# Moving the seams between MLP pieces and attention work in a two-layer transformer kernel

## The reference, cut to what matters

```python
# x: 32 x 64 tokens of 512 (seen as 2048 tokens, 16 tiles of 128); cond: one vector for each of the 32 entries
def layer0(x):
    h = ada_rms(x, cond, ln1)              # x * rsqrt(mean(x^2)) * w * (1 + cond @ tw.T)
    q, k, v = h @ Wq.T, h @ Wk.T, h @ Wv.T # 8 heads of 64, one shared key and value head; rope on q and k
    x = x + softmax(q k^T / 8) v @ Wo.T    # attention inside an entry of 64 tokens
    h = ada_rms(x, cond, ln2)
    return x + (silu(h @ Wg.T) * (h @ Wu.T)) @ Wd.T        # inner width 2048
def layer1(x):
    h = layernorm(x) * (1 + scale(cond)) + shift(cond)
    q = h @ Wq.T; k, v = (h @ Wkd.T) @ Wku.T, (h @ Wkd.T) @ Wvu.T    # 16 heads of 32, 4 key heads, rope
    return x + softmax(q k^T / sqrt(32)) v @ Wo.T
out = layer1(layer0(x))
```

## Time and profile before

| | us |
|---|---|
| median of 3 runs | 886.98 (885.87 to 887.53) |
| the profiled execution, its own time | 887.57 |
| its span from first to last instruction | 885.7 |
| PE busy | 852.0 |
| DVE busy | 631.7 |
| ACT busy | 447.2 |
| POOL busy | 406.6 |

### The profile page before, as it was taken

How to read it: one execution, slowest core, us unless ns; L and a number is a source line. 1 busy time by engine, 2 the same in 40 slices (tenths; PEclk the granted TensorE clock), 3 DMA queues, 4 the chain that set the end, 5 groups by cost and what they waited for, 6 DMA issues and landing times.

```text
span 885.7 us, 15530 instructions
## 1 busy us (share of the span) xinstructions
PE 852.0 (96%) x5864; PEld 707.2 (80%) x5864; DVE 631.7 (71%) x1005; ACT 447.2 (50%) x821; POOL 406.6 (46%) x304
## 2 busy tenths in 40 slices
PE   9798999999999999999989899999999999999997
PEld 6686888788788888787878678788888888888885
DVE  6686577677666677677546877887877867868886
ACT  4665444544444444445445564563553654644662
POOL 2456445545545545537444644544534534431331
PEclk9899999999999999999999899999999999999999
DMA  9811535435425435334423446355354354330001
GB/s 348 330 32 37 172 99 159 124 110 160 122 87 168 122 104 154 116 99 151 156 96 90 169 122 185 115 166 156 121 164 139 114 175 142 117 102 13 25 27 36
DMA packets 114298, 113.54 MB, mean 128 GB/s; under 512 B 57520, under 2 KB 80048, under 8 KB 114224
## 3 DMA queue, kind: packets, MB, share of 16 engines
q1 hardware_dynamic: 113504, 112.45, 39.8%
q10 hardware_dynamic: 720, 0.09, 0.1%
HBM read 88.15 MB, written 24.38 MB: 127 GB/s over the span
## 4 chain that ended last, share of the span: by engine, by line
PE 65%; DVE 11%; ACT 9%; issue 8%; POOL 6%; POOLq 0%; DVEq 0%; ACTq 0%
PE ps L643 20%; PE ps L645 19%; PE ps L644 19%; PE ps L757 2%; POOL gul L511 2%; ACT yf L1763 1%; PE ps L918 1%; ACT L1643 1%; POOL wdl L516 1%; DVE al L1247 1%; DVE ex L1232 1%; PE ps L689 1%; DVE af L1265 1%; ACT ah L1710 1%; ACT guh L1688 1%
## 5 line engine op out<-in xcount | busy, mean ns | idle before, releaser
L511 POOL TENSOR_TENSOR gul<-rgu,guh 128x1024 fp32r<-128x1024 f32 x64 | 154.3, 2411 | 217.5 <-ACT guh L1688 217.5
L1252 DVE TENSOR_TENSOR xres<-ps,xres 128x512 f32<-128x512 f32 x256 | 174.3, 687 | 67.3 <-PE ps L645 67.3
L643 PE MATMUL ps<-h2h,guh 128*128 128x512 f32 x512 | 205.0, 400 | 2.1 <-issue 2.1
L645 PE MATMUL ps<-h2l,guh 128*128 128x512 f32 x512 | 200.6, 392 | 0.0
L644 PE MATMUL ps<-h2h,gul 128*128 128x512 f32 x512 | 200.2, 391 | 0.0
L643 PE MATMUL ps<-wdh,ah 128*128 128x512 f32 x256 | 102.3, 399 | 14.7 <-DVE al L1247 14.7
L643 PEld LDWEIGHTS ps<-h2h,guh 128*128 128x128 f32 x512 | 96.5, 189 | 23.1 <-issue 2.5
L645 PEld LDWEIGHTS ps<-h2l,guh 128*128 128x128 f32 x512 | 96.5, 188 | 21.1
L1710 ACT CAST ah<-af 128x512 fp32r<-128x512 f32 x64 | 39.8, 621 | 143.8 <-DVE af L1265 138.2
L644 PEld LDWEIGHTS ps<-h2h,gul 128*128 128x128 f32 x512 | 96.5, 189 | 19.6
L644 PE MATMUL ps<-wdh,al 128*128 128x512 f32 x256 | 100.7, 393 | 0.0
(11 more groups left out here) (180 smaller groups left out, 1655.5 us busy)
## 6 DMA issues: line engine op xcount, KB each, us to landing
rgu<-gu SPq DMA_DIRECT2D x64, 512.0 KB, 3.9
rwd<-WdT SPq DMA_DIRECT2D x64, 256.0 KB, 3.7
turned_q<-tq SPq DMA_DIRECT2D x20, 320.0 KB, 2.3
qkT<-turned_q SPq DMA_DIRECT2D x20, 320.0 KB, 3.7
turned_p<-tp SPq DMA_DIRECT2D x9, 512.0 KB, 2.6
pT<-turned_p SPq DMA_DIRECT2D x9, 512.0 KB, 3.8
xt<-xT SPq DMA_DIRECT2D x16, 256.0 KB, 2.7
out<-xres SPq DMA_DIRECT2D x15, 256.0 KB, 4.1
```

The lines of the kernel that those rows point to most:

```text
L511: pool.tensor_tensor(gul[i][:, :], rgu[i][:, :], guh[i][:, :], ALU.subtract).then_inc(m_gul, 1)
L643: pe.matmul(dst, lh, rh, start=start, stop=False)
L645: return pe.matmul(dst, lh, rl, start=False, stop=stop)
L1252: dve.tensor_tensor(at, bank(BD[i % 2]), at, ALU.add).then_inc(m_x, 1)
```

## The change

`FILL0[5]` becomes (2, 4, 4) and `FILL1[9]` becomes (4, 0, 0, 0, 0), so each step's work stands two pieces earlier in the order of pieces, and the order across a seam becomes C D | A B. In layer 1, `stats1` moves to the end of the step before, `mean_rstd` to the middle of the first fill on DVE, `rstd1` to the head of the step on POOL, and softmax's scaling and `turn_probs1` behind the whole first fill. `turn_y` goes before `add_x` and `add_out`. The norm of the next MLP tile (`rstd2`, `square2`, `mean_sq2`, `norm2`), `scale_h2` and the trio `scale_shift_y`, `high_y`, `low_y` move before the fourth fill (`norm2` behind it). Layer 0's loop itself is as before, SP's too.

```diff
-FILL0 = {s: (4, 4, 4) for s in range(5, 16)}
-FILL1 = {-1: (4, 4, 0, 4, 0), **{u: (4, 2, 2, 2, 2) for u in range(0, 9)}, 9: (2, 0, 0, 0, 0)}
+FILL0 = {5: (2, 4, 4), **{s: (4, 4, 4) for s in range(6, 16)}}
+FILL1 = {-1: (4, 4, 0, 4, 0), **{u: (4, 2, 2, 2, 2) for u in range(0, 9)}, 9: (4, 0, 0, 0, 0)}
...
@@ POOL, layer 1
-                fill(pieces, min(f1, 2))
                 if u < TAIL:
                     rstd1(u + 2)
-                fill(pieces, f1 - min(f1, 2))
+                fill(pieces, f1)
...
                 fill(pieces, f2 + f3)
-                fill(pieces, f4)
+                if soon is not None:
+                    rstd2(soon)
                 if in_layer(u + 2):
                     low_y(u + 2)
+                fill(pieces, f4)
                 if ready is not None:
                     low_h2(ready)
-                if soon is not None:
-                    rstd2(soon)
                 if u == -1:
                     low_w1_out()
...
@@ DVE, end of layer 0's loop
+                if s == NT - 1:
+                    stats1(1)
@@ DVE, layer 1
-                if u < TAIL:
-                    stats1(u + 2)
                 fill(pieces, min(f1, 2))
                 if in_layer(u):
                     softmax_sums1(u)
+                if u < TAIL:
+                    mean_rstd(u + 2)
+                fill(pieces, f1 - min(f1, 2))
                 if 0 <= u <= TAIL:
                     softmax_scale1(u)
                 if 0 <= u < TAIL:
                     turn_probs1(u)
-                if u < TAIL:
-                    mean_rstd(u + 2)
-                fill(pieces, f1 - min(f1, 2))
...
+                if u < TAIL:
+                    turn_y(u + 2)
                 if u == -1:
                     add_x(NT - 1)
                 if in_layer(u - 1):
                     add_out(u - 1)
-                if u < TAIL:
-                    turn_y(u + 2)
...
-                fill(pieces, f4)
                 if ready is not None:
                     scale_h2(ready)
                 if soon is not None:
                     mean_sq2(soon)
+                fill(pieces, f4)
+                if u < TAIL:
+                    stats1(u + 3)
                 fill(pieces, f5)
                 if u == TAIL - 1:
-                    stats1(u + 3)
                     mean_rstd(u + 3)
@@ ACT, layer 1
-                fill(pieces, f4)
+                if soon is not None:
+                    square2(soon)
                 if u < TAIL:
                     scale_shift_y(u + 2)
                     high_y(u + 2)
+                fill(pieces, f4)
                 if ready is not None:
                     high_h2(ready)
                 if soon is not None:
-                    square2(soon)
+                    norm2(soon)
                 if u == -1:
                     high_w1_out()
                 fill(pieces, f5)
-                if soon is not None:
-                    norm2(soon)
```

## The result

The kernel after takes 896.14 us (median of 5 runs, 892.34 to 901.74) where the kernel before takes 886.63 us in 5 runs beside them. The ratio is 1.0123, 95% interval 1.0077 to 1.0169: slower, and 2.1 us above the upper end of the range. The profiled execution took 896.14 us with a span of 894.3 us, so 8.6 us of span have to be found.

The account below looks back on a forecast made before the run. PE was busy 852.0 of 885.7 us, leaving only its waits and slow clock to win. Terms 4.0 + 0.8 - 0.8 - 1.2 + 0.6 - 2.5 - 0.4 = +0.5 us took the median from 886.98 to 887.5; range 881.5 to 894.

Parts of the forecast that it names:

- Layer 0: Layer 0's eight steps with a norm: late norm makes 9.4 us of 5.3, +4.0 us, and late probabilities add 0.8.
- first rival: Layer 0: the late norm is no loss and the 5.3 us come back, giving 878.2 us; chance 0.1.
- the probabilities: Layer 0's eight steps: their write goes behind weight loads and lands after 4.5 us, 0.1 us a step, +0.8 us.
- third rival: Layer 0: probabilities land later behind the weights, PE waits 1 us per step at the context, 894.7 us; chance 0.15.
- s = 15 and u = -1: Last seam of layer 0 and the one after: less idle PE, -0.8 us at s = 15, -1.2 at u = -1.
- u = 0: Layer 1 seam: waits at gate, additions and context plus a likely clock fall, 7.5 us for 6.9, +0.6 us.
- u = 1 and 2: Layer 1 seams: no `w1` work and `stats1` out of the way, 1.0 us lost for 3.6, -2.5 us.
- u = 3: Layer 1 from this step on: PE is full and the Silu still ends before the next gate, 0 us.
- fourth rival: Layer 1 from u = 1 on: the y chain misses the gate, 0.7 us in 7 steps, 892.4 us; chance 0.12.
- u = 9: Layer 1's tail step: `qkv1(10)` waits less for `af` of the last unit, -0.4 us.

Follow-up runs that it names:

- e3: The kernel after with layer 0's `rstd2` before the last piece of the step (before its `gul`) on GpSimd; ratio 0.9978 to the kernel before, span 882.9 us.
- e4: The kernel after with layer 1's four transfers of turned y and queries ahead of the second weight loads in SyncE's queue; ratio 1.0052 to the kernel before.
- e9: The kernel before with only the two fill tables of the kernel after; ratio 1.0079 to the kernel before, span 892.1 us.
- e10: The kernel after with only layer 1's two writes (turned y, queries) ahead of the weight loads, reads still behind; ratio 1.0132 to the kernel before.
- e7: e5 with tile 12's norm early: `rstd2` before the last `gul` of s = 15, `norm2` before `scale_shift_y(0)`; ratio 0.9884 to the kernel before, median 876.61 us.
- e8: e5 with `low_w1_queries` of s = 14 behind `wdl` of the next piece on GpSimd; ratio 0.9943 to the kernel before, median 880.67 us.
- e6: e5 with layer 1's `mean_rstd(u + 2)` moved behind `turn_probs1(u)` on VectorE; ratio 0.9875 to the kernel before, median 874.97 us.
- e1: The kernel before with only layer 0's seams moved, layer 1 as before; ratio 1.0061 to the kernel before, span 891.3 us.
- e5: The kernel after with the edits of e3 and e4 together; ratio 0.9883 to the kernel before, median 877.05 us.
- e12: e11 with `stats1(2)` behind `softmax_sums1(0)` instead of at the end of u = -1; ratio 0.9853 to the kernel before, median 872.54 us.
- e2: The kernel after with layer 0's old seams, so only layer 1 is changed; ratio 1.0036 to the kernel before, span 886.5 us.
- e11: The kernel after with the edits of e3, e4, e6 and e7 together; ratio 0.9859 to the kernel before, median 873.03 us.

## Why the prediction was wrong

**Layer 0: right, mechanism and nearly size (+5.8 for +4.8).** `stat` 2.2 us later, steps of 33.7 to 34.7, the wait at `xres` in all eight steps. Predicted 0.72 + 0.45 = 1.17 a step; s = 9 takes 1.18 more than s = 10. e3 shows the cause by removing it. The deadline had no slack on either side: the first rival, that the norm might be in time, was one instruction's order away. For the probabilities 0.8 was booked and some 1.8 came, what the eight steps have over 33.74. They land after 4.4 us where 4.5 was said, but they are an event of single steps: PE waits 0.72 us once in after (s = 6), 1.10 once in e4 (s = 13), 0.56, 0.74 and 0.73 in e9, and 0.97, 1.29 and 0.31 in e10. The third rival named the right place; its price, 0.9 in each of 8 steps, was never reached.

**s = 15 and u = -1: half right, -0.8 for -2.0.** The addition of D waits 2.03 us (predicted 2.0), the scores 0.51 (0.75), s = 15 is 0.7 better (0.8). The clock fell behind the 2.03 us gap (0.95 over the 36.49 us, so about 3.6 us at half clock, half of it lost): 0.5 was in the sum and 1.8 came, and u = -1 stayed where it was, 36.49 for 36.54. e7 shows that `turn_x2(12)` behind the y work was the cause of the gap. A wait of 0.85 us for `wdl` behind `low_w1_queries` was not seen; e8 shows that this work costs PE one way or the other.

**u = 0: right in sum, +0.3 for +0.6.** The 1.30 us at the first addition was predicted as 1.3. The 2.9 us expected at the context came instead at the additions before it (2.79), and e6 confirms what caused it: VectorE behind `low_w1_out`. The two places were booked at 0.8 + 2.9 = 3.7 us and came as 2.79 + 0.34 = 3.1, so it is partly luck that the sum is right.

**u = 1 and 2: the step that failed.** The prediction counted VectorE's list, and took "0.3" and "0.7 late" for all that was left. It did weigh the queue of SP, but only for the steps from u = 3, where it found `y_away` at 22.4 us after the scores and the gate still in time. In u = 2 `y_away` left 580.54 - 554.42 = 26.1 us after them. It stood behind `wdl`, which was late itself: its `wdh` followed on ScalarE behind the values, which wait for the rope products on VectorE, behind a scaling of 3.27 us where before had 1.68. The trace shows that chain, but the scaling isn't what counts in it: e4 has the same 3.27 us in its u = 2, and there `wdl` is done 21.9 us after the scores, in after 25.2. In after VectorE had first waited 3.15 us for the Silu at the seam, late behind the y of the step before, so one late y passes its lateness on to the next. y was on ScalarE 34.5 us after the scores (27.4 in e4), where `scale_shift_y` (eight instructions) stands ahead of the Silu and of everything behind it, and the queries, in one queue with y, were late for the next scores. One reordered queue (e4) takes it all away, 33.90 and 33.89 us. Whether the y work put back behind the fourth fill on ScalarE would do the same was not tried. That is the fourth rival's mechanism, "the y chain misses the gate". It was put at 0.7 us in 7 steps with 0.12; it struck in u = 1, 2, 3 and 8 instead, and took with it the 2.5 us that the sum had booked as won. From u = 3 on the estimate was near: `y_away` leaves 22.6 to 23.3 us after the scores, 22.4 was said. What had no term was the same queue in u = 1 and 2. These two steps are 4.7 of the 8.1 us by which the sum was off, u = 3 to 8 are 1.0.

**u = 9: -1.3 for -0.4.** The wait of 0.99 us behind `qkv1(10)` is gone, idle PE fell from 1.43 to 0.43 us.

**The clock at both ends, +1.1 together: not in the sum.** The prediction knew that a gap of 2 us can halve the clock, and counted it for u = -1 and 0 alone. s = 5 has such a gap in every version, the end of the kernel shorter ones, and both got the half clock or not without any change there.

## What to carry to other kernels

When a seam is moved, follow the small instructions on each engine that stand just behind the moved work: a 0.55 us root behind a 2.40 us subtraction cost 1.2 us in eight places. In a queue that mixes weight loads with transfers on the critical path, try the latter first, reads and writes both: here that gave 6.2 us from u = 1 to 4, the writes alone 0.4. And before a difference of 1% is explained, look at the granted clock in the stretches that the change doesn't touch.

## What the runs showed of the hardware that was not expected

**The same gap may or may not cost the clock.** All 14 profiled kernels have an idle PE of 2.06 to 2.09 us before about 84 us, behind the same work. In 8 of them (before, e1, e3, e5 to e8, e12) TensorE then ran at 0.50 for some 3.4 us, in 6 it stayed at 1.00. The wait of 2.8 us at the addition in u = 0 was followed by half clock in after and e4, in e2 and e3 by none. At the end, where PE has only gaps of 0.7 to 1.1 us, one close behind the other, 6 of 14 (after, e5 to e8, e11) had some 6.8 us of half clock, 8 none. The Trainium skill, "TensorE: Matmul & The Clock Gate", part 1, says that the gate's window runs free of the kernel, so that the point of its change varies from run to run. These runs fit that, though none shows the window itself; the prediction read that section as a matter of the gap's length alone. One and the same kernel differs in this too: of the 24 runs of the kernel before beside e1, 22 had a mean clock of 0.988 to 0.990 and took 885.8 to 887.5 us, two had 0.996 and took 882.1.

**VectorE beside GpSimd.** The scaling of layer 1's probabilities reads two SBUF tiles. In the kernel after, where it runs beside `gul`, and in the kernel before (ns, least/median/most):

```profile
L1350 DVE TENSOR_TENSOR ex<-ex,smx x15: 1212/2933/3275, 496.9 to 871.8; 128x1024 f32<-128x1024 f32 x15
```

```profile
L1351 DVE TENSOR_TENSOR ex<-ex,smx x15: 1212/1674/1689, 494.2 to 865.9; 128x1024 f32<-128x1024 f32 x15
```

Alone it takes 1.21 us, beside `gul` 2.9 to 3.3, longer than `gul` itself. By the Trainium skill, "GPSIMD Engine Reference", Key points, such instructions contend; the trace agrees and gives the size. `gul` had started first each time, and the scaling takes its own 1.21 us and nearly all that `gul` had left: 3.27 us with 2.19 left, 2.94 with 1.86, in the kernel before 1.68 with 0.60. It goes the other way round too. In the last five scalings, from 825 us on, the scaling starts first and stays at 1.21 us, and an addition of GpSimd that takes 0.46 us elsewhere takes 1.36 to 1.38:

```profile
825.85 1.38 POOL L549 TENSOR_TENSOR qkr<-u 128x128 f32<-128x128 f32 x1 [6.34 <-DVE u L1316]
```

PE doesn't stop for the slow scaling in u = 1 and 2 of e4; in e8, where the chain was the critical one, a scaling so lengthened took 1.26 us more.
